# Constants of four stages as one array per stage

## What is computed

```python
h = _L0_tok_ref(x, ...)                        # shifted-window attention, 4x4 windows, 8 heads
h = concatenate([cls_tok for each image, h], axis=1)            # 3137 tokens each
h = h + _L0_attn_ref(_layernorm(h), Wq, bq, Wk, ..., norm_scale)    # gated linear memory
h = h + _L0_ffn_ref(_layernorm(h), gate_w, ..., b2)      # 8 experts, top 1, capacity
h = h + _L1_attn_ref(_layernorm(h), W_ih, W_hh, b_ih, b_hh)
        # xp = x @ W_ih.T + b_ih + b_hh;  h_new = tanh(xp_t + h @ W_hh.T)
h = h + _L1_ffn_ref(_layernorm(h), W_fx, b_fx, W_x, b_x, W_slice, b_slice, W_q, W_k, W_v,
                    W_out, b_out, temperature)
        # slice_weights = softmax(((x @ W_x + b_x) @ W_slice + b_slice) / clip(temperature))
```

## Time and profile before

| | us |
|---|---|
| median of 3 runs | 4625.26 |
| lowest, highest | 4613.53, 4629.25 |
| the profiled execution | 4624.52 |
| its span in the profile | 4622.7 |

### The profile page before, as it was taken

The page is one execution under the profiler, slowest core; times in us unless marked ns, Lnnn a source line. Parts: engine busy times, 40 slices in busy tenths (PEclk is TensorE's granted clock), DMA queues, the critical chain, the costliest instruction groups (busy, mean ns, idle before and its releaser), DMA issues. The chain is left out here.

```text
span 4622.7 us, 71095 instructions
## 1 busy us (share of the span) xinstructions
PE 3319.2 (72%) x27016; PEld 1997.0 (43%) x27016; DVE 2487.4 (54%) x3073; ACT 2151.5 (47%) x2829; POOL 2394.7 (52%) x1488
## 2 busy tenths in 40 slices
PE   6999998599999951000069957777567877777786
PEld 5888887255555530000024423333124444444445
DVE  5777776488888864000035524443465655565551
ACT  4666665477777730000024447877123433333343
POOL 3444443377878732777710067774454544454450
PEclk9999999799999965555589968988679988998998
DMA  1111110111111132111033334553111111111111
GB/s 33 36 36 36 38 36 28 30 55 51 53 48 53 54 141 85 44 39 43 24 88 110 105 90 122 131 129 110 33 34 44 41 40 39 53 34 38 44 37 32
DMA packets 300567, 267.46 MB, mean 58 GB/s; under 512 B 104601, under 2 KB 236206, under 8 KB 299216
## 3 DMA queue, kind: packets, MB, share of 16 engines
q1 hardware_dynamic: 264272, 228.39, 16.2%
q0 software_dynamic: 25840, 21.72, 2.7%
q10 hardware_dynamic: 10128, 12.86, 0.7%
HBM read 127.60 MB, written 140.41 MB: 58 GB/s over the span
## 5 line engine op out<-in xcount | busy, mean ns | idle before, releaser
L1489 POOL DMA_INDIRECT D_row<-yb,D_idx x400 | 389.3, 973 | 468.9 <-DMA D_prob<-keepp 347.2
L2129 POOL TENSOR_TENSOR E_hs<-E_w 128x512 f32<-128x512 f32 x200 | 252.9, 1265 | 634.4 <-ACT E_w L1997 634.4
L169 POOL TENSOR_TENSOR A_kmask<-A_ksb,A_head_of_row 128x3584 f32<-128x3584 f32 x56 | 352.4, 6294 | 416.3 <-ACT A_ksb L286 416.3
L1997 ACT ACTIVATE E_w<-E_w 128x1024 f32<-128x1024 f32 x200 | 211.3, 1057 | 646.0 <-DVE E_w L2081 646.0
L1283 PE MATMUL X_px<-X_ident,X_xs 128*128 128x128 f32 x256 | 42.9, 291 | 589.9 <-DMA X_xs<-xb 589.9
L1209 POOL DMA_INDIRECT xb<-S_row,S_idx x400 | 388.8, 972 | 135.3 <-issue 121.5
L2074 DVE TENSOR_REDUCE E_mx<-E_lg 128x16 f32<-128x1024 f32 x200 | 244.4, 1222 | 331.8 <-PE E_lg L1868 331.6
L2135 POOL TENSOR_TENSOR E_w<-E_w,E_rs 128x1024 f32<-128x1024 f32 x200 | 380.5, 1903 | 72.2 <-DVE E_rs L2059 72.2
L231 PEld LDWEIGHTS A_v<-A_wv,A_xrep 128*128 128x128 f32 x3136 | 371.7, 192 | 51.6 <-issue 51.6
L1342 ACT ACTIVATE X_hm<-X_ph,X_b 128x512 f32<-128x512 f32 x128 | 88.0, 688 | 636.6 <-PE X_ph L1295 636.6
L231 PE MATMUL A_v<-A_wv,A_xrep 128*128 128x128 f32 x3136 | 383.0, 277 | 0.0
(11 more groups left out here) (312 smaller groups left out, 7824.4 us busy)
## 6 DMA issues: line engine op xcount, KB each, us to landing
xb<-R_zero SPq DMA_DIRECT2D x8, 2048.0 KB, 22.7
X_xs<-xb SPq DMA_DIRECT2D x64, 256.0 KB, 2.8
yb<-X_ys SPq DMA_DIRECT2D x64, 256.0 KB, 2.0
B_x<-h SPq DMA_DIRECT2D x25, 512.0 KB, 4.4
h<-B_hh SPq DMA_DIRECT2D x25, 512.0 KB, 3.6
y<-B_yt SPq DMA_DIRECT2D x25, 512.0 KB, 2.6
S_row<-y SPq DMA_DIRECT2D x25, 512.0 KB, 3.3
A_xg<-in_xw SPq DMA_DIRECT2D x56, 224.0 KB, 2.5
```

The source lines that it names most:

```text
L169: nc.gpsimd.tensor_tensor(kmask[i % 2][:], bc(ksb[i % 2][:].unsqueeze(2), [128, J, H, Q]), bc(head_of_row[:].unsqueeze(1).unsqueeze(3), [1 ...
L1489: pool.indirect_dma_start(out=row[n % LR][:, k, b], out_offset=None, in_=yb, in_offset=bass.IndirectOffsetOnAxis(ap=idx[:, c, i:i + 1], ax ...
L2129: TT(hs[g % 2][:], w4[:, :, 0], w4[:, :, 1], ALU.add).then_inc(hs_done, 1)
```

## The change

The host lays out the constants of each of the stages A, B, D and E as one array with a row for each partition (stage E: one of 65 rows and one of 128). Block-diagonal zeros, doubled halves, the position pieces and the bias and ones rows of wfa are in the array. The kernel loads it with one DMA (E: two) into one tile, and the old names become column slices of it. The arrays are 128 x 1021 (a), 128 x 1440 (b), 128 x 580 (d), 65 x 2649 (e) and 128 x 129 (f) numbers of 4 bytes, or 523, 737, 297, 689 and 66 KB (KB of 1000 bytes). The memsets of the weights go away. In B and D the array stands behind the first input or table loads on SP and no longer waits for DVE; in A and E it is the first load. In A only the writes to h0 still wait for DVE's memset. In E the host also transposes wx, so eight PE transposes and one ACT copy go away. Routing, dispatch and experts are as before.

```diff
+PACK = {
+    "a": (("wq", 128), ("wk", 128), ("wv", 128), ("wo", 128), ("bq", 1), ("bk", 1), ("bv", 1), ("bo", 1), ("clst", 1),
+          ("head_of_row", H), ("vmask", 128), ("winmask", 2 * (2 * NW // 4) * Q), ("ident", 128), ("pos", Q)),
+    "b": tuple((n, 128) for n in ("q", "k", "v", "i", "f", "o", "mean", "same", "ident", "upto", "center"))
+    + tuple(("b" + n, 1) for n in "qkvifo") + (("ibias", 1), ("scale", 1), ("gate", 2 * E), ("gateb", E)),
+    "d": (("ident", 128), ("mean", 128), ("center", 128), ("wih", 128), ("whh", D), ("b1", 1), ("b2", 1),
+          ("part", 1), ("one", 1)),
+    "e": (("sel", 128), ("wxt", SH * (D + 1)), ("wsl", G), ("unit", D + 1), ("bsl", SH * G), ("temp", SH),
+          ("wfa", SH * (D + 1)), ("wqt", 2 * D), ("wvt", 2 * D), ("wkt", D), ("wout", SH * D)),
+    "f": (("ident", 128), ("bo", 1)),
+}
+
+
+def columns(stage):
+
+    got, k = {}, 0
+    for name, n in PACK[stage]:
+        got[name] = slice(k, k + n)
+        k += n
+    return got, k
+
+
...
+
+        where, width = columns(stage)
+        tile = self.sb("pack_" + stage, [rows, width])
+        return tile, {n: tile[:, k] for n, k in where.items()}
 
...
             def _(sp):
-                sp.wait_ge(memz, 1)
-                for b in range(2):
-                    r = slice(64 * b, 64 * b + 64)
-                    for t, w in enumerate((wq, wk, wv)):
-                        sp.dma_start(w[r, r], a["w1"][t]).then_inc(consts, 16)
-                    sp.dma_start(wo[r, r], a["w2"]).then_inc(consts, 16)
-                    for t, w in enumerate((bq, bk, bv)):
-                        sp.dma_start(w[r, :], a["b1"][t].unsqueeze(1)).then_inc(consts, 16)
-                    sp.dma_start(bo[r, :], a["b2"].unsqueeze(1)).then_inc(consts, 16)
-                    sp.dma_start(clst[r, :], a["cls"].unsqueeze(1)).then_inc(consts, 16)
-                sp.dma_start(head_of_row[:], a["c_head_of_row"]).then_inc(consts, 16)
-                sp.dma_start(vmask[:], a["c_vmask"]).then_inc(consts, 16)
-                sp.dma_start(winmask[:], a["c_winmask"]).then_inc(consts, 16)
-                sp.dma_start(ident[:], a["c_ident"]).then_inc(consts, 16)
-                for qi in range(WS):
-                    for qj in range(WS):
-                        sp.dma_start(pos[WS * qi + qj:128:Q, :],
-                                     bc(a["pos"][3 - qi:7 - qi, 3 - qj:7 - qj].unsqueeze(0),
-                                        [128 // Q, WS, WS])).then_inc(consts, 16)
+                sp.dma_start(pack[:], a["pack_a"]).then_inc(consts, 16)
                 for i in range(S):
                     u = i % 2
                     if i >= 2:
...
                     sp.dma_start(xg[u][:], a["xw"][i]).then_inc(x_in[u], 16)
                     if i == 1:
                         sp.wait_ge(consts, 16 * NCONST)
+                        sp.wait_ge(memz, 1)
                         for p in range(PAIRS):
                             with nc.allow_non_contiguous_dma(reason="one column"):
                                 sp.dma_start(h0[p, :, 0:1], clst[:]).then_inc(edges, 16)
...
...
             def _(dve):
                 V = nc.vector
                 TT = V.tensor_tensor
-                for w in (wq, wk, wv, zero, *qbd):
+                for w in qbd:
                     V.memset(w[:], 0.0)
-                V.memset(wo[:], 0.0).then_inc(memz, 1)
+                V.memset(zero[:], 0.0).then_inc(memz, 1)
                 dve.wait_ge(consts, 16 * NCONST)
                 V.tensor_scalar(bqs[:], bq[:], HE ** -0.5, None, ALU.mult)
...
-        loads = []
-        for s in HALF:
-            for n, src in (("q", a["m_Wq"]), ("k", a["m_Wk"]), ("v", a["m_Wv"])):
-                loads += [(wts[n][s, d], src) for d in HALF]
-                loads += [(bias[n][s, :], a["m_b" + n].unsqueeze(1))]
-            for j, n in enumerate("ifo"):
-                loads += [(wts[n][s, d], a["m_Wg"][:, D * j:D * j + D]) for d in HALF]
-                loads += [(bias[n][s, :], a["m_bg"][D * j:D * j + D].unsqueeze(1))]
-            loads += [(center[s, d], a["c_center"][0:D, 0:D]) for d in HALF]
-            loads += [(ibias[s, :], a["m_input_bias"].unsqueeze(1)), (scale[s, :], a["m_norm_scale"].unsqueeze(1))]
-        for b in range(2):
-            loads += [(gate[HALF[b], E * b:E * b + E], a["e_gate_w"])]
-        loads += [(gateb[:], a["e_gate_b"].partition_broadcast(128))]
-        loads += [(mean[:], a["c_mean"]), (same[:], a["c_same"]), (ident[:], a["c_ident"]), (upto[:], a["c_upto"])]
-        CN = 16 * len(loads)
+        CN = 16
         m.open()
...
                 load(0)
+                sp.dma_start(pack[:], a["pack_b"]).then_inc(consts, 16)
                 load(1)
-                sp.wait_ge(memz, 1)
-                spread(nc, sp, loads, consts)
                 for t in range(CHUNKS + 4):
...
                 V = nc.vector
                 TT, TS, STT = V.tensor_tensor, V.tensor_scalar, V.scalar_tensor_tensor
                 scan, copy = V.tensor_tensor_scan, V.tensor_copy
-                for t in (gate, mem, mems, lf, cml, nl, drop):
+                for t in (mem, mems, lf, cml, nl, drop):
                     V.memset(t[:], 0.0)
                 V.memset(keep[:], 1.0)
...
                 sp.dma_start(idx[:], gidx.rearrange("c p b -> p c b")).then_inc(tables, 16)
                 sp.dma_start(prob[:], keepp.rearrange("c p b -> p c b")).then_inc(tables, 16)
+                sp.dma_start(pack[:], a["pack_d"]).then_inc(consts, 16)
                 load(0)
                 load(1)
-                sp.wait_ge(memz, 1)
-                spread(nc, sp, loads, consts)
                 for t in range(N + 6):
                     at(load, t + 2)
                     at(keep_k, t - 5)
...
                 TT = V.tensor_tensor
                 V.memset(eps[:], EPS)
-                V.memset(wih[:], 0.0).then_inc(memz, 1)
                 dve.wait_ge(consts, CN)
                 TT(b1[:], b1[:], b2[:], ALU.add).then_inc(ready, 1)
                 dve.wait_ge(tables, 32)
...
             @block.sync
             def _(sp):
+                sp.dma_start(pack[:], a["pack_e"]).then_inc(consts, 16)
+                sp.dma_start(wide[:], a["pack_f"]).then_inc(consts, 16)
+
                 def cols(j):
                     return slice(W * j, min(W * j + W, TP))
 
...
 
                 for j in range(3):
                     load_y(0, j)
-                spread(nc, sp, loads, consts)
                 for it, n, c in schedule():
...
                 pe.wait_ge(consts, CN)
                 pe.wait_ge(fixed, 1)
-                for h in range(SH):
-                    last = turn(WT[0:G, 512 * (h // 4) + K1 * (h % 4):512 * (h // 4) + K1 * (h % 4) + K1],
-                                wxa[:, G * h:G * h + G], ident[0:K1, 0:K1])
-                last.then_inc(pre, 1)
-                pe.wait_ge(turned, 1)
                 for h in range(SH):
                     mm(O[0:K1, G * h:G * h + G], wxt[:, h], wsl[:], start=True, stop=False, skip_group_check=True)
                     mm(O[0:K1, G * h:G * h + G], unit[:], bsl[:, h], start=False, stop=True, skip_group_check=True)
...
                 nc.scalar.preload_act_table_set(TANH)
                 act.wait_ge(pre, 1)
-                A(wxt[:].rearrange("p (x h) c -> p x (h c)", x=2),
-                  WT[0:D, :].rearrange("p (x r) -> p x r", x=2)[:, :, 0:4 * K1], ACT.Copy).then_inc(turned, 1)
-                act.wait_ge(pre, 2)
                 for b in range(2):
                     A(amat[HALF[b], HALF[b]], Z[HALF[b], 0:D], ACT.Copy).then_inc(copied, 1)
                     A(bmat[HALF[b]], WT[HALF[b], BANK[1]].rearrange("p (q x d) -> p q x d", x=2, d=D)[:, :, b], ACT.Copy).then_inc(copied, 1)
                 A(wfx[:].rearrange("p (x h) c -> p x (h c)", x=2),
                   LG[0][:].rearrange("p (x r) -> p x r", x=2)[:, :, 0:4 * K1], ACT.Copy).then_inc(copied, 1)
-                act.wait_ge(pre, 3)
+                act.wait_ge(pre, 2)
                 A(wxs[:], LG[1][:, BANK[0]], ACT.Copy).then_inc(copied, 1)
 
                 for it, n, c in schedule():
...
                 V = nc.vector
                 TT, TS, STT = V.tensor_tensor, V.tensor_scalar, V.scalar_tensor_tensor
-                V.memset(wfa[0:D, :, D:K1], 0.0)
-                V.memset(amat[:], 0.0)
+                V.memset(amat[:], 0.0).then_inc(fixed, 1)
                 dve.wait_ge(consts, CN)
-                V.memset(wfa[D:K1, :, D:K1], 1.0).then_inc(fixed, 1)
                 TS(temp[:], temp[:], 0.1, 5.0, ALU.max, ALU.min).then_inc(fixed, 1)
                 dve.wait_ge(fixed, 2)
                 V.reciprocal(rtemp[:], temp[:]).then_inc(fixed, 1)
                 dve.wait_ge(fixed, 3)
-                dve.wait_ge(pre, 2)
+                dve.wait_ge(pre, 1)
                 TT(wxp[:].rearrange("p (h g) -> p h g", h=SH), O[0:K1, :].rearrange("p (h g) -> p h g", h=SH),
```

(26 more changed lines are left out.)

114 lines of the change are left out of this document (62 added, 52 removed).

## The result

The changed kernel takes 4549.18 us (median of 4 runs, 4541.68 to 4557.34). The kernel before takes 4625.47 in the same comparison (4613.53 to 4629.25). The ratio is 0.984, with a 95% interval of 0.9815 to 0.9864. The forecast was 4553. Every ratio and interval here is the recorded one, taken over the runs in the fast state, and can differ by some 0.1% from the quotient of two medians.

What follows compares the result with a forecast made beforehand. The prediction took serial issue of many small transfers on SP to bound the stage heads. Gains of 25.0 (A), 33.5 (B), 0 (D) and 13.1 (E) sum to 71.6 us: 4624.5 - 71.6 = 4552.9, or 4553; 8-in-10 range 4543 to 4574.

Steps and rivals of the forecast that it cites:

- 1.75 us: In the stage heads: fixed part of a load's landing time, to which all bytes up to its end at 325 GB/s are added.

## What to carry over

A stage's head that waits for a sum of small loads costs about one issue for each load, 0.63 us in A ((29.63 - 5.79) / 38); lay the constants out on the host in the tile's form and load them with one DMA behind the first input tile. Lay such an array over all 128 rows where you can: 1.4 MB in 128 rows came within 0.5 us of 0.75 MB in 65 and 128, and 0.75 MB in 128 rows (stage A) came after 4.4 us, not 6.2. Avoid a number of rows like 67, a prime: that load took 31 us and held three later issues of the queue for 4 to 13 us. Before packing a head, look whether a larger load is nearly as late: in stage D and in routing the gain was about 1 us, though 13 and 4 small loads became one.

## What the runs showed of the hardware

- After 1.75 us, loads of 128 rows moved at 285 to 350 GB/s, one of 65 rows at 170 (its small companion of 128 rows included), one of 67 rows at 24. The 67 rows went one packet at a time, the 65 rows 13 and the 128 rows 16 at a time, and the packets of the 65 rows took 0.71 us instead of 0.40 to 0.42.
- POOL's masking operation on 128 x 3584 numbers took 6294 ns with its small operand in a tile of its own, 6358 with it at column 517 of an array, 6295 at column 512. DVE's eviction took 688 ns at columns 525 and 528, as with a tile of its own.
- The same kernel took 4616 us on one chip and 4796 on another. Nearly all of it was in stage D, which gathers rows: 572 against 747 us, at a granted clock of 0.85 against 0.76 and 116 against 90 GB/s. Every head agreed to 0.2 us. On a third chip it took 4788 us. POOL, which issues the gathers, was no busier (389 against 383 us); what made them slower is open.
